# Scales in two buffers, y copied into the product buffer, one band of ones, and the first mask ahead of the states

## The reference

```python
bc = einsum('bti,oi->bto', value, W_bc).reshape(B, T, H, 4, N)
bc = bc / (sqrt(sum(bc * bc, axis=-1, keepdims=True)) + EPS)
Bz, Bx, Cz, Cx = bc[..., 0, :], bc[..., 1, :], bc[..., 2, :], bc[..., 3, :]
def step(z, s):
    S = 1 / (1 + dt * k + dt * dt * A)
    z = S * (z - dt * A * s + dt * (Bz * u))
    s = s + dt * z + dt * (Bx * u)
    y = Cz . z + Cx . s
out = ((y + skip * value) * silu(gate)) @ W_out.T
```

## Time and profile before

| | |
|---|---|
| three runs | 2394.12, 2403.24, 2406.58 us, median 2403.24 |
| profiled execution | 2401.71 us, its span 2400.0 us |
| busy: TensorE, VectorE, ScalarE, GpSimd | 2009.4, 1911.9, 932.8, 311.4 us |
| mean granted clock of TensorE | 0.894 |
| phases (start of L1136 to the next), the first 14 | 102.7 to 114.4 us, mean 107.8 |

### The profile page before, as it was taken

The page is one execution under the profiler, slowest core; times in us unless marked ns, Lnnn a source line. Parts: engine busy times, 40 slices in busy tenths (PEclk is TensorE's granted clock), DMA queues, the critical chain, the costliest instruction groups (busy, mean ns, idle before and its releaser), DMA issues. The chain is left out here.

```text
span 2400.0 us, 73278 instructions
## 1 busy us (share of the span) xinstructions
PE 2009.4 (84%) x29474; PEld 1234.3 (51%) x29474; DVE 1911.9 (80%) x4411; ACT 932.8 (39%) x1913; POOL 311.4 (13%) x588
## 2 busy tenths in 40 slices
PE   5776294898999899898989898998989897828896
PEld 2333142465555555464555555465555556726775
DVE  5776445989798987978897898989798889538885
ACT  3555231343435333343435343343424342205554
POOL 0000111111121211111221111111121111000000
PEclk9888697899999999898999998899989996559999
DMA  3555653364544535344544545464545433073410
GB/s 95 165 174 166 164 140 95 101 157 115 134 134 138 139 111 145 114 125 124 151 118 130 148 123 130 114 153 113 134 134 135 127 108 93 14 216 138 169 64 27
DMA packets 231278, 304.40 MB, mean 127 GB/s; under 512 B 115744, under 2 KB 132128, under 8 KB 222752
## 3 DMA queue, kind: packets, MB, share of 16 engines
q1 hardware_dynamic: 123968, 148.65, 21.7%
q10 hardware_dynamic: 86368, 96.50, 14.1%
q0 software_dynamic: 20608, 54.56, 8.9%
HBM read 240.85 MB, written 57.68 MB: 124 GB/s over the span
## 5 line engine op out<-in xcount | busy, mean ns | idle before, releaser
L695 PE MATMUL m_ps_a<-m_valT,m_w_bc 128*128 128x512 f32 x2048 | 1011.8, 636 | 56.6 <-DMA m_valT<-scratch_valT 39.3
L695 PEld LDWEIGHTS m_ps_a<-m_valT,m_w_bc 128*128 128x128 f32 x2048 | 385.9, 200 | 455.5 <-issue 438.0
L644 POOL DMA_DIRECT2D m_shear<-scratch_shear x512 | 273.1, 534 | 1294.2 <-DVE m_psi L1020 1183.7
L834 ACT ACTIVATE m_sq<-m_ps_a 128x512 f32<-128x512 f32 x256 | 152.9, 597 | 548.5 <-PE m_ps_a L695 548.5
L1020 DVE TENSOR_TENSOR m_psi<-m_psi,m_prod 128x128 f32<-128x128 f32 x1024 | 295.5, 289 | 20.2
L1016 DVE TENSOR_TENSOR m_prod<-m_psi,m_shear 128x128 f32<-128x128 f32 x1024 | 292.6, 286 | 16.9 <-issue 1.1
L756 PE MATMUL m_ps_g<-m_raw 32*64 32x64 f32 x8192 | 177.8, 243 | 105.6 <-DVE m_g L1125 83.1
L756 PEld LDWEIGHTS m_ps_g<-m_raw 32*64 32x64 f32 x8192 | 157.4, 154 | 188.4 <-issue 183.9
L1080 DVE TENSOR_TENSOR m_part<-m_raw,m_psi 128x1024 f32<-128x1024 f32 x128 | 155.8, 1220 | 22.2 <-issue 21.2
L1043 DVE TENSOR_TENSOR m_raw<-m_raw,m_scale 128x1024 f32<-128x1024 f32 x64 | 78.2, 1223 | 114.5 <-DMA m_scale<-scratch_norm 112.4
L224 PE MATMUL ps_w<-p_xnT,w_in 128*128 128x512 f32 x256 | 129.8, 660 | 40.3 <-ACT vraw L282 34.9
(11 more groups left out here) (154 smaller groups left out, 2713.0 us busy)
## 6 DMA issues: line engine op xcount, KB each, us to landing
m_scale<-scratch_norm SPq DMA_DIRECT2D x512, 128.0 KB
m_w_bc<-in_w_bcT ACTq DMA_DIRECT2D x252, 256.0 KB, 3.5
m_shear<-scratch_shear POOLq DMA_DIRECT2D x512, 64.0 KB, 2.9
m_det<-scratch_ab POOLq DMA_DIRECT2D x64, 256.0 KB, 6.2
scratch_yT<-m_y ACTq DMA_DIRECT2D x64, 224.0 KB, 2.4
scratch_gateT<-gate SPq DMA_DIRECT2D x8, 1024.0 KB, 3.9
scratch_valT<-val SPq DMA_DIRECT2D x8, 1024.0 KB, 4.4
scratch_svgT<-svg SPq DMA_DIRECT2D x8, 1024.0 KB, 5.7
```

Of the source, the lines that this page charges most:

```text
L644: pool.dma_start(shear[h * N:(h + 1) * N, w % 2].rearrange("p k g t -> p k (g t)"), spread(src)).then_inc(into.sem, into.step)
L695: mm = pe.matmul(ps_a[j % 2].ap(), w_bc[:, j, kt, :], valT[:, kt, :], start=(kt == 0), stop=(kt == KI - 1))
L834: act.activation(sq[:, j, :], ps_a[j % 2].ap(), ACT.Square).then_inc(sq_ready.sem, sq_ready.step)
```

## The change

- `scale` has two buffers, `[P, 2, 2, T]`: the loads for the inputs go into the first and wait for `b_scaled` of the group before, those for the outputs go into the second and wait for `c_scaled` of the group before. SP issues all eight loads in a row. `load_e_end` moves behind them, `load_valT` stands between n1 and n2.
- y is copied into `raw[0:112, group, 3, :]`, which the group's queries no longer need, and stored from there. The copy no longer waits for the store of the group before. ScalarE's copy of a product into slot 3 waits for the store made from it a row earlier.
- `of_segment` is replaced by `band`, 39 columns in which four, eight columns apart, hold the ones of the four heads; segment s reads 32 columns from column 7 - s on. One copy of ScalarE fills it in place of eight.
- The order of a phase on VectorE is: keys 1, scales n0, keys 2, in n0, out n0, scans, keys 3, scales n1, queries 0, queries 1, mask 0, coefficients, states, mask 1, queries 2, in n1, out n1, scales n2, queries 3, mask 2, in n2, out n2, scales n3, the steps left, mask 3, in n3, out n3, keys of n0.

The diff, without the renaming of semaphores and buffers in the declarations:

```diff
-        scale = sb("scale", [P, 2, T])
+        scale = sb("scale", [P, 2, 2, T])
-        y = sb("y", [ROWS, T])
-                        sp.dma_start(scale[h * N:(h + 1) * N, :, :], spread(src)).then_inc(scale_in.sem, scale_in.step)
+                        sp.dma_start(scale[h * N:(h + 1) * N, half, :, :], spread(src)).then_inc(scale_in[half].sem, scale_in[half].step)
 def input_scales(b, group):
     ...
     sp.wait_ge(rows_stored.sem, rows_stored.at(b, group))
-    sp.wait_ge(c_scaled.sem, c_scaled.at(b, group - 1))
+    sp.wait_ge(b_scaled.sem, b_scaled.at(b, group - 1))
     load_scales(group % 2, 0)
 def output_scales(b, group):
-    sp.wait_ge(b_scaled.sem, b_scaled.at(b, group))
+    sp.wait_ge(c_scaled.sem, c_scaled.at(b, group - 1))
     load_scales(group % 2, 1)
 # SP, one phase
-                            norm_rows(b, then)
-                            input_scales(b, then)
-                            load_e_end(b, half + 1)
-                            output_scales(b, then)
-                            norm_rows(b, then + 1)
-                            input_scales(b, then + 1)
-                            output_scales(b, then + 1)
-                            norm_rows(b, then + 2)
-                            input_scales(b, then + 2)
+                            for i in range(2):
+                                norm_rows(b, then + i)
+                                input_scales(b, then + i)
+                                output_scales(b, then + i)
+                                if i == 0:
+                                    load_e_end(b, half + 1)
                         if half == 0 and not last:
                             load_valT(b + 1)
                         if more:
-                            output_scales(b, then + 2)
-                            norm_rows(b, then + 3)
-                            input_scales(b, then + 3)
-                            output_scales(b, then + 3)
+                            for i in range(2, HALF):
+                                norm_rows(b, then + i)
+                                input_scales(b, then + i)
+                                output_scales(b, then + i)
 # TensorE
-  ... of_segment[:, s, :], sq[:, j, s * SEG:(s + 1) * SEG],
+  ... band[:, N // HP - 1 - s:N // HP - 1 - s + N], sq[:, j, s * SEG:(s + 1) * SEG],
 # ScalarE
-                for s in range(N // HP):
-                    act.activation(of_segment[:, s, s::N // HP], head_sum[:, 0:HP], ACT.Copy).then_inc(segments_ready, 1)
+                act.activation(band[:, N // HP - 1::N // HP], head_sum[:, 0:HP], ACT.Copy).then_inc(band_ready, 1)
                     act.wait_ge(y_made.sem, y_made.at(b, group - HG))
+                    if j == NJ - 1:
+                        stored = y_stored[group % HALF]
+                        act.wait_ge(stored.sem, stored.at(b, group // HALF - 2))
-                    act.dma_start(dram["yT"][b, group, 0:ROWS, :], y.ap()).then_inc(y_stored.sem, y_stored.step)
+                    act.dma_start(dram["yT"][b, group, 0:ROWS, :], raw[0:ROWS, group, 3, :]).then_inc(stored.sem, stored.step)
-                    act.wait_ge(y_stored.sem, y_stored.at(b, group - 1))
-                        act.activation(chunks(y.ap())[:, odd::2, :],
+                        act.activation(chunks(raw[0:ROWS, group, 3, :])[:, odd::2, :],
 # VectorE, states
-                        if c == NC // 2 - 1:
-                            between()
 # VectorE, one phase
                     if more:
                         scale_inputs(b, then, advance)
+                        scale_outputs(b, then, advance)
                     det_sums(b, half, advance)
+                    keys(b, first + 3, advance)
                     if more:
-                        scale_outputs(b, then, advance)
                         scales(b, then + 1, advance)
-                    keys(b, first + 3, advance)
-                    queries(b, first, advance)
+                    queries(b, first + 0, advance)
+                    queries(b, first + 1, advance)
+                    mask(b, first + 0, advance)
+                    coefficients(b, half, advance)
+                    states(b, half, advance)
+                    mask(b, first + 1, advance)
+                    queries(b, first + 2, advance)
                     if more:
                         scale_inputs(b, then + 1, advance)
-                    queries(b, first + 1, advance)
+                        scale_outputs(b, then + 1, advance)
                     if more:
-                        scale_outputs(b, then + 1, advance)
                         scales(b, then + 2, advance)
-                    coefficients(b, half, advance)
-                    states(b, half, advance, lambda: mask(b, first, advance))
-                    if more:
-                        scale_inputs(b, then + 2, advance)
-                    queries(b, first + 2, advance)
-                    mask(b, first + 1, advance)
-                    if more:
-                        scale_outputs(b, then + 2, advance)
-                        scales(b, then + 3, advance)
                     queries(b, first + 3, advance)
                     mask(b, first + 2, advance)
                     if more:
-                        scale_inputs(b, then + 3, advance)
+                        scale_inputs(b, then + 2, advance)
+                        scale_outputs(b, then + 2, advance)
+                    if more:
+                        scales(b, then + 3, advance)
                     advance(OF_PHASE)
                     mask(b, first + 3, advance)
                     if more:
+                        scale_inputs(b, then + 3, advance)
                         scale_outputs(b, then + 3, advance)
                         keys(b, then, stepping(b, half + 2, not last))
```

More of the change, by code:

```diff
@@ L455, in mix @@
         head_sum = sb("head_sum", [P, N])
-        of_segment = sb("of_segment", [P, N // HP, N])
+        band = sb("band", [P, N // HP - 1 + N])
         causal = sb("causal", [P, C])
@@ L504, in mix @@
         rows_stored = sig("rows_stored", HG, 16)
-        scale_in = sig("scale_in", HG * 2 * HP, 16)
+        scale_in = [sig(f"scale_in{n}", HG * HP, 16) for n in range(2)]
         a_made = sig("a_made", UNITS)
@@ L531, in mix @@
         y_ready = sig("y_ready", HG * 2)
-        y_stored = sig("y_stored", HG, 16)
+        y_stored = [sig(f"y_stored{s}", 2, 16) for s in range(HALF)]
         narrow_next = sem("narrow_next")
@@ L553, in _ @@
                     sp.dma_start(w_bc[:, j, :, :].rearrange("p k m -> p (k m)"), a["w_bcT"][0, j]).then_inc(w_in[j].sem, w_in[j].step)
-                for s in (factor_in, rows_stored, scale_in):
+                for s in (factor_in, rows_stored, *scale_in):
                     sp.sem_inc(s.sem, s.given * s.step)
@@ L956, in _ @@
                 over_rows(act, body)
-                act.wait_ge(y_stored.sem, y_stored.at(B - 1, HG - 1))
+                for stored in y_stored:
+                    act.wait_ge(stored.sem, stored.at(B - 1, 1))
             @block.vector
@@ L963, in _ @@
                     dve.sem_inc(s.sem, s.given * s.step)
-                dve.memset(of_segment.ap(), 0.0).then_inc(const_set, 1)
+                dve.memset(band.ap(), 0.0).then_inc(const_set, 1)
                 dve.memset(one.ap(), 1.0).then_inc(const_set, 1)
@@ L1040, in scale_inputs @@
                     dve.wait_ge(raw_ready.sem, raw_ready.at(b, group * NJ + 1))
-                    dve.wait_ge(scale_in.sem, scale_in.at(b, (group * 2 + 1) * HP - 1))
+                    dve.wait_ge(scale_in[0].sem, scale_in[0].at(b, (group + 1) * HP - 1))
                     v = raw[:, group % HG, 0:2, :]
-                    dve.tensor_tensor(v, v, scale.ap(), ALU.mult).then_inc(b_scaled.sem, b_scaled.step)
+                    dve.tensor_tensor(v, v, scale[:, 0], ALU.mult).then_inc(b_scaled.sem, b_scaled.step)
                     advance(ns(2 * T))
@@ L1048, in scale_outputs @@
                     dve.wait_ge(raw_ready.sem, raw_ready.at(b, group * NJ + 3))
-                    dve.wait_ge(scale_in.sem, scale_in.at(b, (group * 2 + 2) * HP - 1))
+                    dve.wait_ge(scale_in[1].sem, scale_in[1].at(b, (group + 1) * HP - 1))
                     v = raw[:, group % HG, 2:4, :]
-                    dve.tensor_tensor(v, v, scale.ap(), ALU.mult).then_inc(c_scaled.sem, c_scaled.step)
+                    dve.tensor_tensor(v, v, scale[:, 1], ALU.mult).then_inc(c_scaled.sem, c_scaled.step)
                     advance(ns(2 * T))
@@ L1146, in coefficients, with states @@
                         advance(ns(28))
-                def states(b, half, advance, between):
+                def states(b, half, advance):
                     dve.wait_ge(dX_ready.sem, dX_ready.at(b, (half + 1) * HALF * 2 - 1))
```

8 lines of the change are left out of this document (4 added, 4 removed).

## The result

The changed kernel takes 2526.2 us (median of 2514.2, 2525.3, 2527.0 and 2529.6) against 2402.1 for the kernel before: a ratio of 1.0507, 95% interval 1.0466 to 1.0549. It is slower, as forecast, and by more: +124 us where +82 was forecast, inside the range of 2415 to 2550.

A forecast was written before the change was run, and what follows sets the result against it. VectorE's work plus its waits for scales was taken as the bound: 2401.7 us profiled, +93.6 net over 15 phases, -12.6 prologue, +1 last phase, 2484 us. Range 2440 to 2550 (chance 0.63), with the crowd's case 2415 to 2550.

The forecast's parts named there:

- VectorE's work plus its waits is the length of a phase: Middle stage: VectorE's work (94.3 us of a 105 us phase) plus its waits for scales sets the phase length.
- TensorE the bound: Rival, chance 0.06: TensorE's 83.1 us wait for the first mask sets the phase; the earlier mask gives it back, 2306 us.
- a wait that only TensorE has is slack: Middle stage: waits of TensorE alone, such as 83.1 us for a mask, do not lengthen a phase.
- Out loads behind the in loads, 2.5 us: Scale loads: output scales usable 2.5 us after input scales instead of 5.7; prologue saves 12.6 us.
- pays in full: Rival, chance 0.05: loads land within their cover, all out waits go and no in wait comes, 2357 us.
- nothing bought: Rival, chance 0.05: despite the second buffer, out still starts 5.7 us after in, 2624 us.
- the crowd stays away: Rival, chance 0.12: the m_det loads do not delay n2's scales, n2 loses 3.2 + 1.0 us a phase, 2421 us.
- all terms low: Rival, chance 0.09: every term near its low end, 2403 us, no change.
- n2 inherits n3's wait: n2's scales, now ahead of the last queries among the m_det loads: in wait 3.2 us a phase (2.5 to 4.2).
- n3, 4.4 us for in and 1.4 for out: n3's scales at the phase end, 4.0 us of cover: waits 4.4 (3.1 to 6.5) and 1.4 (0.8 to 2.6).
- First mask, 1.0 us: First mask, now ahead of the states: VectorE waits 1.0 us a phase (0 to 3.4) for TensorE's scores.
- y, band, queues: y in raw's slot, the one band of ones, and the order of SP's queue: each costs nothing.

The follow-up runs named there:

- e2: e1 plus the two scale buffers with all eight loads in a row, in VectorE's order of the kernel before: 2372.6 us, ratio 0.9856.
- e5: Changed kernel with ScalarE's det_inverses moved behind copy_terms of the third group instead of the second: 2488.5 us, ratio 1.0347.
- e6: Changed kernel with the m_det loads after the first half cut to one of four groups: 2463.3 us, ratio 1.0245.
- e9: e2 with n0's input and output scales placed behind the four scans on VectorE: 2330.8 us, ratio 0.9722.
- e3: e2 with the first mask moved ahead of the coefficients and states: 2385.7 us, ratio 0.9920.
- e7: Kernel before with the m_det loads after the first half cut to one of four groups: 2362.7 us, ratio 0.9830.
- e10: e9 with n3's input and output scales moved into the next phase, behind its first keys, likewise in the prologue: 2339.7 us, ratio 0.9729.
- e4: Changed kernel with one scale buffer instead of two and SP's order in a phase as in the kernel before: 2833.5 us, ratio 1.1775.
- e1: Kernel before with only y in the product buffer and the one band of ones: 2403.0 us, ratio 0.9997.
- e8: Changed kernel with VectorE reordered so that each scale load has at least 9 us of other work: 2428.0 us, ratio 1.0090.

## Why the prediction was right, and where it was short

- *VectorE's work plus its waits is the length of a phase.* It holds for before, the changed kernel, e2, e5, e6 and e9. The rival (TensorE the bound) fell with e3, which gives TensorE its mask and gains nothing. But the step ends sooner than the prediction had it: at the last mask 27 of 73 us that were gained came back (e7), and once n0's wait was gone, all of it (e10). The half sentence behind it, that a wait which only TensorE has is slack, is where the account broke; see the first mask.
- *Out loads behind the in loads, 2.5 us.* In to out was 2.4 us at n0 and 2.7 at n2; the transposes of the first keys came 11.6 us sooner (418.35 to 406.73), of 12.6 forecast. The rivals fell one by one: TensorE as the bound with e3; pays in full with the 97 us that n3 waited (15 x 6.5); nothing bought with e2, and with the out waits of e4, 309.1 us against 51.6; the crowd stays away with the 44.5 us of n2, which e6 takes off; and all terms low with n2, n3 and the first mask, which lay 0.5 to 3.1 us above their low ends.
- *n2 inherits n3's wait.* 3.0 us against 3.2, and e6 and e7 show the cause.
- *n3, 4.4 us for in and 1.4 for out.* 4.2 and 2.3: the distance from L1034 to L1042 was 8.4 us on average, as taken. That it fits so closely is in part luck: the 8.4 came from 11 distances at n0, but all 15 of them waited, and their mean is 8.6. The out term was undersized by 0.9 a phase, 13 us in all: in to out was 3.5 us there, not 2.5. What the out loads of n3 share the engines with I did not test. It is not m_det: with that cut (e6) the distance stays 3.5. In the phase shown GpSimd issues four loads of shear from 859.50, and the DMA share is 0.96 from 861 to 865.
- *First mask, 1.0 us.* The step that failed. It measured 3.1 a phase, 31 us more than the forecast term. That this lies within the bound of 3.4 is luck: the bound came from the time at which the scores ended before, not from the chain that made the wait. The reason written for the low value was that TensorE, freed of its wait, would be less late. The prediction also had TensorE wait "for the keys that end a phase: nothing". What the runs showed: ScalarE's program ties TensorE to VectorE's scans, and the moved scales delayed these; with ScalarE's inverses behind the copies the masks' wait falls from 48.8 to 8.5 us (e5). The prediction read the scans of n0 only as a cover that the out scales lose. That the scans themselves now stand behind the out scales and their wait, that ScalarE waits for them with the keys' copies queued behind, and that TensorE waits for those, was in no step of it, though ScalarE's 17.3 us of waiting for the scans already stood in the waits of the kernel before.
- *y, band, queues.* Nothing, as said (e1). The order of SP was costed at nothing in the right direction, but e4 shows that it hangs on VectorE's order: `load_valT` behind n2's loads costs TensorE 176 us of waiting (214.0 against 37.9).
- *The signs.* In waits 180.7 (some 180), out waits 51.6 (near 50), n3's in 4.2 (about 4) and TensorE's wait for the mask 8.9 (near nothing) came as said; VectorE's work in a phase is 94.7 us (94.3). The new wait for the keys did not come in the changed kernel. Phases take 111.2 to 122.4 us, mean 115.8 (111 to 114). The sign for being wrong, TensorE's busy share above 90% of a phase, told nothing: it is 90.1 and 90.5% in two of the first 14 phases, and was above that in 7 of 14 before.
- *The sum.* Forecast 2484, first mask +31, n3's out +13, the small terms of n0, n2 and n3's in together -10: 2518, against 2514.2 profiled. The other 12 us up to the median of 2526.2 are the distance of this execution from the median of its kernel, 0.5%, where the kernel before had 0.06%.

By parts: y and band 0, buffers -30, mask first +13, the new places +140. Of these, 38 hang on the chain through the inverses; n3, whose loads are now covered by 4.2 us of work, waits 97 in all, and n2 pays what n3 paid before.

## What to carry to other kernels

When a round trip through DRAM waits on a chain (compute, store, wait, load, use), list for each use the work between the last link and the use, in microseconds, before and after a reordering. A second buffer takes off only the part of the chain that was serialised by the buffer. Here that was 3.4 to 4.3 us between a group's in and out (e4 against the changed kernel at n0, n2 and n3); the 8 to 9 us from the scales to the in stayed, and the new order left less work to cover them.

When an operation moves, ask also which in-order engine waits for it and what stands behind that wait. ScalarE's wait for the scans came to 17 us in all before, and to 135 us once the scans had moved behind a wait and TensorE had lost one.

When two engines each have 94 us of work in a phase of 101, as in e9, removing more waits from one can move them to the other (e10). From there on, shorten work.

## What was not expected of the hardware

- Of two loads of 512 KB (4 pieces each) issued in a row, the second was used 2.4 us behind the first at n0 and 2.7 at n2 (2.4 and 2.8 where it was waited for). Issued only when the first has been used, it was used 5.8 to 7.2 us behind it (e4). So issuing in a row takes 3.4 us off at n0, 4.3 at n2 and 3.7 at n3. At n3 the two in a row stood 3.5 us apart, which is not explained. The Trainium skill (DMA: Bandwidth & Descriptors, Anatomy of one DMA) has, for DMAs issued from GpSimd, 2.0 us fixed and bytes over 436 GB/s; an estimate from that is 1.2 us between the two. These loads are issued from SP, and no run here has the second waited for less than 2.0 us behind the first (e8).
- Beside 1 MB of other loads the same 512 KB took 12.7 us from the scales (L1034) to use, and 9.6 or less with that cut to 256 KB (e6). The DMA engines' share read 1.05 in that stretch.
